# First stage of a two-layer graph network: moments in three groups, later key turns, zeroing on ScalarE, first chunk loads ahead of the weights

## What is computed

```python
h = jnp.maximum(_layernorm(x, axis=-1), 0.0)
q = (h @ Wq + bq).reshape(N, DH, NH)
k = (h @ Wk + bk).reshape(N, DH, NH)
v = k
scores = jnp.einsum('edh,edh->eh', q[rows], k[cols])
m = jax.ops.segment_max(scores, rows, num_segments=N)
ex = jnp.exp(scores - m[rows])
denom = jax.ops.segment_sum(ex, rows, num_segments=N)
attn = ex / denom[rows]
msgs = attn[:, None, :] * v[cols]
out = jax.ops.segment_sum(msgs, rows, num_segments=N)
x = x + out.reshape(N, HIDDEN) @ Wo + bo
...
h = jnp.maximum(_layernorm(x, axis=-1), 0.0)
agg = jax.ops.segment_sum(h[src], dst, num_segments=N)
ah = agg / in_deg[:, None]
x = x + h @ W1.T + b1 + ah @ W2.T + b2
```

## Time and profile before

| | |
|---|---|
| median of 3 runs | 1931.77 us (1930.68 to 1932.28) |
| profiled execution, its own time | 1932.3 us |
| its span, first to last instruction | 1930.5 us |
| mean granted TensorE clock | 0.949 |
| TensorE busy | 1666.8 us, 86% of the span |
| VectorE busy | 1336.3 us, 69% |
| ScalarE busy | 1001.1 us, 52% |
| GpSimd busy | 1141.1 us, 59% |
| TensorE in the chain that ended last | 51%, VectorE 20% |

### The profile page before, as it was taken

The page is one execution under the profiler, slowest core; times in us unless marked ns, Lnnn a source line. Parts: engine busy times, 40 slices in busy tenths (PEclk is TensorE's granted clock), DMA queues, the critical chain, the costliest instruction groups (busy, mean ns, idle before and its releaser), DMA issues.

```text
span 1930.5 us, 24219 instructions
## 1 busy us (share of the span) xinstructions
PE 1666.8 (86%) x5735; PEld 963.8 (50%) x5735; DVE 1336.3 (69%) x2587; ACT 1001.1 (52%) x3779; POOL 1141.1 (59%) x1323
## 2 busy tenths in 40 slices
PE   3799863688988889898888897895999999999998
PEld 1344331466666666666666666342444444444443
DVE  8768994888888989898988885465444444444441
ACT  4453313499999999999999997241000000000000
POOL 2000001878787878888787880013777777777773
PEclk9899876799999989999999999997999999999999
DMA  8122104665657565665657562945777777777774
GB/s 188 52 69 71 63 28 145 192 168 143 192 150 190 160 184 170 168 186 163 191 149 197 145 179 61 222 109 153 210 217 212 219 218 219 216 214 211 215 213 140
DMA packets 133201, 318.07 MB, mean 165 GB/s; under 512 B 41908, under 2 KB 42158, under 8 KB 133044
## 3 DMA queue, kind: packets, MB, share of 16 engines
q0 software_dynamic: 70240, 229.93, 41.8%
q1 hardware_dynamic: 62804, 86.44, 16.2%
HBM read 280.43 MB, written 35.86 MB: 164 GB/s over the span
## 4 chain that ended last, share of the span: by engine, by line
PE 51%; DVE 20%; issue 15%; POOL 7%; DMA 4%; ACT 2%; DVEq 1%; SPq 0%; POOLq 0%; ACTq 0%
PE wide L769 14%; PE sums L929 12%; PE sums L832 12%; PE wide L860 9%; POOL arena L504 7%; DVE nodes L1338 2%; DVE arena L1083 2%; DVE arena L1082 2%; DMA h2tab<-node 2%; DVE nodes L1284 1%; DVE nodes L1329 1%; DVE node L1225 1%; PE wide L782 1%; PE wide L787 1%; ACT arena L582 1%
## 5 line engine op out<-in xcount | busy, mean ns | idle before, releaser
L636 ACT ACTIVATE nodes<-arena,nodes 128x64 f32<-128x64 f32 x2840 | 682.7, 332 | 1.2 <-PE sums L832 1.2
L504 POOL DMA_INDIRECT arena<-ktab,idx x425 | 421.5, 992 | 188.1 <-issue 142.2
L504 POOL DMA_INDIRECT arena<-h2tab,idx x425 | 445.7, 1049 | 135.8 <-issue 134.9
L832 PE MATMUL sums<-nodes,oh 128*125 128x260 f32 x1768 | 466.7, 407 | 47.0 <-DVE nodes L1284 47.0
L769 PE MATMUL wide<-w_sb,node 128*125 128x512 f32 x1000 | 465.6, 610 | 20.7 <-ACT node L567 12.3
L832 PEld LDWEIGHTS sums<-nodes,oh 128*125 128x125 f32 x1768 | 342.0, 198 | 123.3 <-DVE nodes L1284 58.4
L929 PE MATMUL sums<-arena,oh 128*125 128x512 f32 x850 | 375.9, 600 | 6.9 <-DMA arena<-h2tab,idx 6.5
L716 ACT ACTIVATE node<-wide 128x500 f32<-128x500 f32 x51 | 27.3, 585 | 570.9 <-PE wide L915 570.8
L860 PE MATMUL wide<-q_win,node 125*128 125x512 bf16 x1275 | 310.3, 381 | 3.0 <-issue 3.0
L769 PEld LDWEIGHTS wide<-w_sb,node 128*125 128x125 f32 x1000 | 187.0, 193 | 230.8 <-issue 201.8
L1329 DVE TENSOR_TENSOR nodes<-wide,arena 128x1024 f32<-128x1024 f32 (+1 forms) x225 | 258.6, 1159 | 12.4 <-PE wide L860 11.8
(11 more groups left out here) (202 smaller groups left out, 1165.9 us busy)
## 6 DMA issues: line engine op xcount, KB each, us to landing
node<-node_tab SPq DMA_DIRECT2D x27, 531.2 KB
q_win<-qtab SPq DMA_DIRECT2D x26, 336.0 KB
arena<-ktab,idx POOLq DMA_INDIRECT x425, 5.1
arena<-h2tab,idx POOLq DMA_INDIRECT x425, 3.9
h2tab<-node POOLq DMA_DIRECT2D x25, 250.0 KB, 2.7
node<-h2tab SPq DMA_DIRECT2D x26, 224.0 KB
qtab<-q_win SPq DMA_DIRECT2D x17, 336.0 KB
nodes<-x SPq DMA_DIRECT2D x5, 1120.0 KB
```

Source lines behind the costliest of these rows:

```text
L504: gp.indirect_dma_start(rows[:, b, t, :], None, tab, bass.IndirectOffsetOnAxis(ap=idx[:, b, t:t + 1], axis=0)).then_inc(s["rows_in"][b][PA ...
L636: last = act.activation(msgs[:, t, h // HH, h % HH * DH:(h % HH + 1) * DH], rows[:, 1 - b, t, h * DH:(h + 1) * DH], ACT.Copy, scale=den_in ...
L832: last = pe.matmul(halves[:, u, :], oh[:, 1 - b, t, :], rhs[side][:, t, u, :], start=t == 0, stop=t == CT - 1)
```

## The change

- `moments` and `normed` work on three groups, x group 0, x group 1, and x groups 2 to 4 at once (`NORMS`). Group 0's moments come right behind the key products, ahead of the signs; its norm ahead of the sort. Group 1's moments follow phase 3 and its norm phase 4; group 2's follow phases 5 and 8.
- ScalarE's `norm` is split: the root is taken in the turn of tile 1 or 6 (`ROOTS_AT`), and the wait for the norm stands at tile 3 or 8, ahead of the first row that needs it (`NORM_AT`).
- `COUNTED` is 5 instead of 20, so counting runs to tile 14 and `totals` stands after tile 16.
- GpSimd's zeroing goes; ScalarE zeroes in nine passes in tiles 15 to 23 (`zero_part`).
- The key turns stand ahead of tiles 22, 23 and 24, and the fourth behind tile 24's last `leave`; before, ahead of tiles 20 to 23.
- SyncE stores the chunk table ahead of its wait for the last tile's store, and loads the first two chunks and the first Q window ahead of `Wo` and `W1T`.

```diff
-        COUNTED = 20
+        COUNTED = 5
+        NORMS = [(0, 1), (1, 2), (2, XG)]
+        ROOTS_AT, NORM_AT = {1: 1, 6: 2}, {3: 1, 8: 2}
...
-        QK_TURNS = [NW - 5, NW - 4, NW - 3, NW - 2]
+        QK_TURNS = [NW - 3, NW - 2, NW - 1]
...
-            stored_qk(NW - 1)
-
-            sp.wait_ge(s1["k_ready"], NW)
-            for k, n in enumerate(("Wo", "W1T")):
-                sp.dma_start(w_sb[:, k, :, :], io[n].rearrange("(c p) d -> p c d", p=128)).then_inc(w_in, 16)
...
-                sp.wait_ge(tabs_done, j * 16 + 16)
             store_table(0)
+            stored_qk(NW - 1)
...
+            sp.wait_ge(tabs_done, 16)
             sp.wait_ge(stored_keys[0], 32)
             sp.wait_ge(stored_nodes, 16)
...
             load_q(0, 0)
 
+            sp.wait_ge(s1["k_ready"], NW)
+            for k, n in enumerate(("Wo", "W1T")):
+                sp.dma_start(w_sb[:, k, :, :], io[n].rearrange("(c p) d -> p c d", p=128)).then_inc(w_in, 16)
...
-            gp.memset(rows[:, 1, :, :], 0.0).then_inc(pool_step, 1)
-            gp.memset(oh[:, 1, :, :], 0.0).then_inc(pool_step, 1)
-            gp.wait_ge(pool_step, 9 + 1 + 2 + 1 + 2)
-            gp.sem_inc(consts, 1)
...
+            def zero_part(n):
+
+                if n < ZERO_PARTS:
+                    size = CT * D // ZERO_PARTS
+                    act.activation(last_rows[:, n * size:(n + 1) * size], zero[:, 0:1].to_broadcast([128, size]), ACT.Copy).then_inc(zeroed, 1)
+                elif n == ZERO_PARTS:
+                    act.activation(last_oh, zero[:, 0:1].to_broadcast([128, CT * WIN]), ACT.Copy).then_inc(zeroed, 1)
...
             for t in range(NW):
-                if (t + 4) % XT == 0 and t + 4 < NW:
-                    norm((t + 4) // XT)
+                if t in ROOTS_AT:
+                    roots(ROOTS_AT[t])
                 if t + 1 < NW:
                     cols(t + 1)
+                if t in NORM_AT:
+                    act.wait_ge(norm_ready, NORM_AT[t] + 1)
                 if t + 2 < NW:
                     row(t + 2)
...
                 if t < (2 * NW - COUNTED) // 3:
                     count_sides(3)
+                else:
+                    zero_part(t - (2 * NW - COUNTED) // 3)
...
+            moments(0)
             then(dve.tensor_copy(ones_row[:, :], zero[0:BR, 0:1].to_broadcast([BR, 128])))
...
+            normed(0)
...
+            between = {3: lambda: moments(1), 4: lambda: normed(1), 5: lambda: moments(2), 8: lambda: normed(2)}
             for k in range(1, CB):
                 inner_phase(k)
+                if k in between:
+                    between[k]()
...
-            gaps = {CB + 2: ready_group(3), CB + 4: ready_group(4), CB + 5: (find_totals, lambda: None)}
...
-            dve.wait_ge(consts, 3)
+            dve.wait_ge(zeroed, 8 + 1)
```

More of the change, by code:

```diff
@@ L553, in _, with roots @@
         def _(act):
-            def norm(n):
-                group = rstd[:, n * XT:(n + 1) * XT]
+            def roots(n):
+                group = rstd[:, NORMS[n][0] * XT:NORMS[n][1] * XT]
                 act.wait_ge(var_ready, n + 1)
                 act.activation(group, group, ACT.Sqrt).then_inc(std_ready, 1)
-                act.wait_ge(norm_ready, n + 1)
             def relu(t, b, i, s):
@@ L602, in third_part @@
                 act.activation(part_stage[t % STAGES][:, 2, :], wide[t % 2][0:WIN, 0:D], ACT.Copy).then_inc(s1["out_ready"], 1)
-            norm(0)
+            last_rows = rows[:, 1, :, :].rearrange("p t d -> p (t d)")
+            last_oh = oh[:, 1, :, :].rearrange("p t n -> p (t n)")
+            ZERO_PARTS = 8
+            def zero_part(n):
[4 more added lines that the diff above has]
+                    act.activation(last_oh, zero[:, 0:1].to_broadcast([128, CT * WIN]), ACT.Copy).then_inc(zeroed, 1)
+            roots(0)
+            act.wait_ge(norm_ready, 1)
             row(0)
@@ L957, in moments @@
             def moments(n):
[L959 to L963 removed]
+                tiles = range(NORMS[n][0] * XT, NORMS[n][1] * XT)
+                for x in range(*NORMS[n]):
+                    dve.wait_ge(x_in[x], 16 * len(ROW_SPLIT))
+                    for t in range(x * XT, (x + 1) * XT):
+                        dve.bn_stats(stats[:, t, :], x_sb[:, t, :]).then_inc(s1["step"], 1)
+                dve.wait_ge(s1["step"], tiles.stop)
+                for t in tiles:
                     last = dve.bn_aggr(mv[:, t, :], stats[:, t, :])
                 then(last)
[L966 removed]
+                group = slice(tiles.start, tiles.stop)
                 dve.tensor_scalar(rstd[:, group], mv[:, group, 1], EPS, None, ALU.add).then_inc(var_ready, 1)
             def normed(n):
[L971 removed]
+                group = slice(NORMS[n][0] * XT, NORMS[n][1] * XT)
                 dve.wait_ge(std_ready, n + 1)
@@ L1166, in inner_phase, with outer_phase @@
                     one.negate_before(k)
-                first, second = after.get(k, (None, None))
-                if first:
-                    first()
-                for bit in reversed(range(k)):
-                    for one in keys:
-                        one.exchange(stride(bit))
-                    if second and bit == k - 1:
-                        second()
+                local_steps(reversed(range(k)))
+            between = {3: lambda: moments(1), 4: lambda: normed(1), 5: lambda: moments(2), 8: lambda: normed(2)}
             for k in range(1, CB):
                 inner_phase(k)
+                if k in between:
+                    between[k]()
             for one in keys:
                 one.sign_before(CB)
-            moments(2)
-            local_steps((8,))
-            normed(2)
-            local_steps((7, 6, 5, 4, 3, 2, 1, 0))
-            def outer_phase(k, turn_in, turn_out, gap=(lambda: None, lambda: None)):
+            local_steps((8, 7, 6, 5, 4, 3, 2, 1, 0))
+            def outer_phase(k, turn_in, turn_out, meanwhile=lambda: None):
                 for one in keys:
                     one.sign_before(k)
-                first, second = gap
-                first()
+                meanwhile()
                 for one in keys:
                     turn_in(one)
-                second()
                 for bit in reversed(range(k - CB)):
```

18 lines of the change are left out of this document (5 added, 13 removed).

## The result

| | before | after |
|---|---|---|
| median | 1932.03 us (1930.68 to 1933.87, 4 runs) | 1888.39 us (1886.53 to 1892.73, 4 runs) |
| profiled execution, its own time | 1932.3 us | 1888.04 us |
| its span | 1930.5 us | 1886.2 us |
| mean granted TensorE clock | 0.949 | 0.960 |

The two spans lie 44.3 us apart. The timelines of VectorE say where: the first decode moved from 332.45 to 292.36, which is 40.1 us; the other 4.2 us came later, in chunks that the change doesn't touch.

A forecast was written before the change was run, and what follows sets the result against it. Sort on VectorE and Q/K tiles on TensorE stop each other, both ending near 305 us, with the first chunk's transfers behind. 1932.3 less 41.3 shift plus 0.5 for weights, less 0.5 to the median: 1891.0 us; range 1886 to 1899.

The forecast's parts named there:

- The stage as two chains that stop each other: First stage: VectorE's sort and TensorE's Q and K tiles halt each other, with waits of 33.4 and up to 14.5 us.
- Start of VectorE: Kernel start: without GpSimd's memsets blocking the shared port, the cast ends at 8.96 instead of 14.07 us, gaining 5.1.
- First rows: After x group 0 lands at 12.6 us: first row near 21, TensorE's first transposes near 23.3 instead of 29.55.
- Waits at the turns: Key turns: VectorE waits 4.0 us at the first and 2.7 at the fourth; TensorE idles 5 before the third.
- Node table and first load: Behind the sort: node table stored at 277.2 us, first chunk's first load at 282.45 instead of 323.75, shift 41.3.
- The weights: Wo and W1T among the first chunk's gathers: push of 0.5 us taken, bounds 0 and 8.0; gathers' rate halved meanwhile.
- (b): Rival at the first chunk: the weights push it by the full 8.0 us, total 1899; chance 0.12.
- All later stages shifted by one amount: Sign of being right: everything behind the first decode, which the change doesn't edit, moves by the same shift, 41.3 us.
- (a): Rival at the start: x group 0 lands at 20.55 and the port stays blocked; about 1896.7 us; chance 0.09.
- (c): Rival in the sort: group 2's root still comes late, VectorE takes first keys at 249; 1917 us; chance 0.03.
- (d): Rival on TensorE: working 215 us in a row drops its clock to the lower level; slower than before; chance 0.02.

The follow-up runs named there:

- e8: Kernel before with only the regrouped moments and roots (twenty counts, GpSimd's zeroing, old turns, old load order kept): 1902.07 us, ratio 0.9839.
- e4: Changed kernel with zeroing again by GpSimd's two memsets at the start and none on ScalarE: ratio 0.9855, first decode at 292.96 us.
- e3: Changed kernel with the four key turns back at their old places, ahead of tiles 20 to 23: ratio 0.9821.
- e6: Changed kernel with every key turn one tile earlier, ahead of tiles 21 to 24: 1882.41 us, ratio 0.9746.
- e12: Changed kernel run again without edit, on a chip with longer chunks: first decode at 293.20 us, 1871.20 us from there to the end.
- e5: Changed kernel run again without edit, for a second trace: 1890.47 us, ratio 0.9787.
- e7: Kernel before with the new load order alone, chunk table and first chunks' loads ahead of the weight loads: 1925.84 us, ratio 0.9965.
- e1: Changed kernel with the old load order, weights ahead of the chunk table and first chunk's loads: ratio 0.986, first decode at 292.08 us.
- e9: e8 with the new load order as the only addition: ratio 0.9815, first decode at 296.70 us.
- e2: Changed kernel with every key turn one tile earlier, the same kernel as e6 in another run: ratio 0.9785, first decode at 286.79 us.
- e10: Changed kernel with twenty counts instead of five ahead of the first root: ratio 0.981, first decode at 292.94 us.
- e11: Kernel before run again without edit, on a chip with longer chunks: first decode at 331.28 us, 1870.62 us from there to the end.

## Why the prediction was right, and where it was off

- **The stage as two chains that stop each other:** right. e8 alone, which regroups the moments, brings 31.0 us. In the changed kernel TensorE has no gap from 50 to 200 us and VectorE no wait for a root (group 2's moments 48.70 to 58.9, forecast 46 to 57; group 2's root done at 82.4, forecast 81, and no wait behind it). Before, TensorE also stood 12.7 us at tile 2, until 63.46, and its clock was at the lower level from 60 to 69 us; both are gone.
- **Start of VectorE:** the mechanism was right, its worth not. The gain of 5.1 us that I booked for the cast (end 8.96 forecast, 9.16 measured) was spent waiting for x. The mis-sized term is the landing of x group 0: 12.6 forecast, 15.47 measured, inside the bounds of 10.1 to 20.55. The even rate over the queue was too kind to its first part: Wq, queued behind x and nearly as large, landed only 1.7 us behind it (3.15 and 14.0), Wk 6.8 us behind Wq. The sum has a slip too. By the sizes of the issues 1.7 of 3.8 MB stand up to x group 0, and 12.6 counts from Wk's issue; from the queue's first issue at 0.72 the even rate gives 10.7. The sort therefore began at 22.62, not near 20. This cost little: the wait for the totals shrank from the forecast 3 us to 1.60, and the first turned keys were wanted at 219.5 (224.04 less 4.51; forecast 219.2). The Trainium skill (SBUF — State Buffer, SBUF: two separate sides) was right on the block, 9.19 to 0.18 us, and that ScalarE's zeroing doesn't bring it back (VectorE's exchanges follow each other every 0.34 us beside the pass at 166.64 as ahead of it). That the block costs the kernel anything is not what the page says, and e4 shows 0.6 us.
- **First rows:** the first transposes stood at 23.97 instead of 23.3. Wk released them, since it took 20.3 us to land and not 19.6, but the late x alone would have held them nearly as long: the first row began at 22.74, not near 21, and transposes follow a row's start by 1.07 us where the row releases them (28.48 and 29.55 before), which is 23.8. In e3, e6 and e12 it is the row that releases them. These 0.7 us go through all of TensorE's chain: turns at 223.40, 233.14, 247.59 and 261.66, forecast 222.6, 232.3, 246.9 and 261.1.
- **Waits at the turns:** 4.51, TensorE's 4.98 and 2.85, forecast 4.0, 5 and 2.7. The slow tile behind the gap cost 1.15 (4.75 against 3.60), forecast 1.5; the prediction took the price from a row and didn't say why there is one, and the windows above show it: the lower clock level. I named the first wait the price of the later turns, and it is: e6 takes it away. The forecast did not ask whether another table of turns would do better.
- **Node table and first load:** store at 278.30, forecast 277.2. Of these 1.1 us 0.6 were there at the fourth turn already; the turn itself was a slow one (1.68 us instead of 1.04), which I had not booked. TensorE had stood 1.17 and 0.69 us in the passes ahead of it, and the clock fell to the lower level within the turn (0.67 on the mean from 261.6 to 262.5, then 0.50). First load 283.70, forecast 282.45, so the shift is 40.1 and not 41.3. Decode 8.66 later, forecast 8.7.
- **The weights:** right in size, 0.5 us forecast and next to nothing found. The DMA issues of the changed kernel and, for the gathers, of 280 to 330 us (count, KB each, median us to landing) answer to the earlier trace rows:

```profile
w_sb<-W1T SPq DMA_DIRECT2D x1, 1024.0 KB, 21.3
```

```profile
arena<-ktab,idx POOLq DMA_INDIRECT x24, 7.4
```

  The collision is there. W1T took 21.3 us to land instead of 8.0, a gather of the first chunks 7.4, where in the same stretch of the kernel before (320 to 370 us) it is this line:

```profile
arena<-ktab,idx POOLq DMA_INDIRECT x24, 5.8
```

  The same stretches of e5, e6 and e7, which have the weights there too, give 7.6, 6.7 and 7.2 us, that of e8, which has not, 5.5. SyncE's next issue took 2.72 us. But the second decode still follows at 22.04. The next chunks take 33.1 and 33.1 us against 32.8 and 32.5 before, yet in e8, where the weights go first, 33.4 and 33.2. The Trainium skill (DMA: Bandwidth & Descriptors, Queues, rings and completion order) has the queues share each engine packet by packet; the trace agrees that gathers slow down, by 1.6 us. The halving was my estimate and came out too large. Rival (b), the 8 us of push, didn't come; the slack in the earlier trace rows is the likely reason, but no run tests it.
- **"All later stages shifted by one amount"** was wrong. The shift was 40.1 at the first decode and 44.3 at the end. This, and nothing in the first stage, put the measured time below the forecast: the terms up to the decode were 1.2 us too hopeful, the later stages gave 4.2 us back (7.4 in the first 25 chunks, less 3.2 behind them). With the 0.5 booked for the weights that is the 3.5 us by which the profiled execution, 1888.04, lies below its forecast of 1891.5. What the forecast owes to its mechanism is the shift of 40.1; that the two errors have opposite signs is luck.
- **The rivals:** (a) came half: x was late by 2.9 us, the port was free, and TensorE lost 0.7. (b) and (c) didn't come. (d) didn't: the clock was 1.00 from 50 to 200 us, and fell only when TensorE had stood.
- **What the prediction did not see** is that parts of the change stand in for each other. The first load of the first chunk by the turns and the load order (us; e8 and e9 also start TensorE 5.7 us later):

| | weights ahead of the loads | loads ahead of the weights |
|---|---|---|
| turns late, early start | 283.62 (e1) | 283.70 (after) |
| turns at old tiles, early start | not run | 283.77 (e3) |
| turns at old tiles, late start | 294.95 (e8) | 287.58 (e9) |

  With late turns TensorE ends its last turn 14 us ahead of the sort's last cast (263.3 and 277.2 in the changed kernel), and the weights fit in between. With old turns they don't, and the new order saves 7.4 us (measured with the late start; the cell that isn't run would say it for the early one). With the new order the turns may stand at either place. The runs of a row or column come from different chips, so half a microsecond between them means little. I had costed the two edits as one sum, and it came out, since the sum followed times through the stage rather than adding a worth for each edit.

## What to carry to other kernels

Follow absolute times through each chain and take the later one at every meeting; the worth of an edit alone (7 to 8 us for the load order in e7) says nothing of its worth on top of others (0 in e1). Where two engines hand work to each other at points that a table sets, a whole table moved by one step is a cheap thing to try: here the middle between the old places and the new ones gave 8 us over the new (e6, e5) and a first decode 5.4 us ahead of the old (e2, e3). Before paying for a faster start, look at what lands last: the cast came 5 us earlier and waited for x.

## What the runs showed of the chip that was not expected

- A gather and 2 MB of plain loads in other queues: median landing 5.8 to 7.4 us for the gathers, 8.0 to 21.3 us for the second load, and SyncE's next issues took 2.72, 2.50 and 2.08 us instead of 0.3 to 0.6.
- A gap of some microseconds on TensorE is paid again behind it, through the clock: eight transposes took 1.97 instead of 1.04 us, and the eight passes after them 4.75 instead of 3.60 (third turn of the changed kernel, 4.98 us of waiting). In e3 and e8 to e10 every turn with a wait of 3.2 us or more took 1.97 us, and the first turn, without a wait, 1.04. In the turns of 1.94 to 1.97 us that were looked at (before, after, e2, e3, e6, e9) the granted clock was 0.50, in those of 1.33 and 1.73 us (before's third, e2's second) 0.77 and 0.73, in before's fourth, 1.04 us, 1.00.
- VectorE's `edge` took 9.19 us beside GpSimd's two memsets in before, e4, e8, e9 and e11, ending with the second, but 7.38 us in e7, ending with the first.
- The granted clock of a stage that the edit never touched differs between kernels: 0.95 over the first 25 chunks of before, e7 and e8, 0.96 in after, e5 and e6. Single chunks took 34.0 to 34.8 us instead of 32.5, and the first 25 took 812.3 to 813.2 us against 805.8 to 807.9; between before and after 3 us of that were lost again behind them (784.8 and 788.0 us to the end).
